# Last stage of a two-layer perceiver block: weights loaded and mixed a stage earlier, values weighted with the masked scores moving, end by batches, bias on VectorE

## The reference

```python
x = x + L0_xattn(layernorm(x), ctx)      # 16 heads over 4096 context tokens
x = x + L0_attn(layernorm(x))            # low-rank attention
x = x + L0_ffn(layernorm(x))             # 16 experts, 4 a token
x = x + L1_xattn(layernorm(x), ctx)      # top-32 attention, film, S4D, feed-forward
x = x + L1_attn(layernorm(x))            # retention, below
x = x + L1_ffn(layernorm(x))             # mixed experts, below
```

```python
# L1_attn: 8 heads of 32
Q, K, V = X @ W_Q, X @ W_K, X @ W_V      # per head
Q, K = xpos(Q), xpos(K, downscale=True)
scores = (Q @ K.T) * decay(n - m), 0 where m > n
Y = scores @ V                           # no softmax
Yn = groupnorm(Y) over each head's 32 features
Yn = Yn * gn_weight + gn_bias
out = silu(X @ W_G) * Yn @ W_O
# L1_ffn
Wsel, bsel = W[ids], b[ids]              # 8 of 32 matrices, 256x256
out = einsum('k,kod,bsd->bso', weights, Wsel, x) + einsum('k,ko->o', weights, bsel)
```

## Time and profile before

| | |
|---|---|
| median of 3 runs | 1250.7 us (1249.63 to 1252.78) |
| profiled execution | 1249.94 us, its span 1248.7 us |
| granted TensorE clock, mean over the span | 0.848 |
| TensorE busy | 1023.1 us, 82% |
| VectorE busy | 835.4 us, 67% |
| ScalarE busy | 627.9 us, 50% |
| GpSimd busy | 253.1 us, 20% |
| last stage | 1142.4 to 1248.7 us |

### The profile page before, as it was taken

The page is one execution under the profiler, slowest core; times in us unless marked ns, Lnnn a source line. Parts: engine busy times, 40 slices in busy tenths (PEclk is TensorE's granted clock), DMA queues, the critical chain, the costliest instruction groups (busy, mean ns, idle before and its releaser), DMA issues. The chain is left out here.

```text
span 1248.7 us, 20560 instructions
## 1 busy us (share of the span) xinstructions
PE 1023.1 (82%) x7560; PEld 624.6 (50%) x7560; DVE 835.4 (67%) x1812; ACT 627.9 (50%) x1014; POOL 253.1 (20%) x276
## 2 busy tenths in 40 slices
PE   6988589999999999868799782587787778973877
PEld 5877434444444444438455461335545456442564
DVE  5677689999999998036334559988485744533472
ACT  4434138787887888613311140799696882011100
POOL 1000488895000000000000010073434330000100
PEclk9999769999999999967799876667877789977855
DMA  6777522223222221010122270014521155003200
GB/s 207 273 260 270 185 66 77 78 77 84 76 76 80 76 76 39 10 53 1 52 89 76 80 187 5 1 56 115 139 78 51 39 156 186 0 1 84 68 1 17
DMA packets 97993, 110.63 MB, mean 89 GB/s; under 512 B 26475, under 2 KB 74404, under 8 KB 97892
## 3 DMA queue, kind: packets, MB, share of 16 engines
q1 hardware_dynamic: 95572, 108.52, 28.9%
q10 hardware_dynamic: 2320, 0.79, 0.3%
HBM read 79.77 MB, written 29.43 MB: 87 GB/s over the span
## 5 line engine op out<-in xcount | busy, mean ns | idle before, releaser
L806 ACT ACTIVATE pT<-bank 128x512 f32<-128x512 f32 x512 | 278.4, 597 | 94.6 <-PE bank L745 73.2
L827 DVE TENSOR_REDUCE rmax<-bank 128x2 f32<-128x1024 f32 x256 | 307.4, 1223 | 19.1 <-PE bank L713 18.1
L1547 PE MATMUL bank<-K1s,qs 97*128 97x512 f32 x256 | 137.2, 629 | 56.0 <-ACT below L1653 36.6
L757 PE MATMUL bank<-pT,V 128*17 128x256 f32 x2048 | 161.8, 388 | 4.7 <-ACT oT L812 4.6
L745 PEld LDWEIGHTS bank<-qs,ks 49*128 49x128 f32 x1024 | 78.1, 187 | 113.8 <-ACT pT L806 100.8
L1810 POOL TENSOR_TENSOR total<-total,work 128x1024 f32<-128x1024 f32 x40 | 94.7, 2375 | 194.9 <-ACT work L1662 194.5
L745 PE MATMUL bank<-qs,ks 49*128 49x256 f32 x1024 | 130.5, 333 | 2.5 <-ACT pT L806 0.5
L713 PE MATMUL bank<-ks,qs 49*128 49x512 f32 x512 | 111.2, 429 | 16.2 <-DMA ks<-k_parts_d 9.0
L1547 PEld LDWEIGHTS bank<-K1s,qs 97*128 97x128 f32 x256 | 61.1, 250 | 72.7 <-ACT below L1653 37.3
L1717 DVE MAX8 cand<-work 128x8 f32<-128x128 f32 x384 | 77.5, 279 | 0.0
L1662 ACT ACTIVATE work<-bank,ebias 128x1024 f32<-128x1024 f32 x48 | 53.6, 1120 | 31.7 <-PE bank L1550 31.7
(11 more groups left out here) (432 smaller groups left out, 1870.2 us busy)
## 6 DMA issues: line engine op xcount, KB each, us to landing
k_parts_d<-kparts SPq DMA_DIRECT2D x48, 512.0 KB, 3.6
ks<-k_parts_d SPq DMA_DIRECT2D x384, 64.0 KB, 2.2
K1s<-k_parts_d SPq DMA_DIRECT2D x96, 128.0 KB
cn<-in_ctx SPq DMA_DIRECT2D x32, 384.0 KB, 3.4
cx<-in_ctx SPq DMA_DIRECT2D x16, 384.0 KB
w<-in_L_ffn_w SPq DMA_DIRECT2D x32, 128.0 KB
w2e<-in_L_ffn_w SPq DMA_DIRECT2D x16, 128.0 KB
W<-in_L_xattn_W SPq DMA_DIRECT2D x2, 1024.0 KB, 7.4
```

The source lines that it names most:

```text
L757: t = pe.matmul(bank[32 * c:32 * c + VW, 7, a * S:(a + 1) * S], V[:, b * NCH + 4 * g + c, h, :], pT[:, (at + 2 * (c // 2) + a) % 8, c % 2 ...
L806: p_made.up(act.activation(pT[:, at % 8, :], bank[:, 4 + at % 3, :], ACT.Exp))
L827: max_read.up(dve.tensor_reduce(rmax[p % 2][:, :, qt, c], bank[:, b0:b0 + 2, :], AX.X, ALU.max))
L1547: m = pe.matmul(bank[:, b0 + c, :], qs1[0:NROW1, b * H1 + h, q], K1s[h][0:NROW1, keys], start=True, stop=(what == "new"))
```

## The change

The tiles of the last stage's loads, masks and mixed weights move to a region of SBUF that the film stage leaves free (the last 53 kB a partition), so that they can be written during it. Two new programs, `ret_load_sync` and `ret_load_pool`, run in the film stage in front of its own functions, and `mix_vector` is called in `film_vector` between the additions of `b2` and the first use of the feed-forward's result. The swapped copies are made by GpSimd. The biases of the experts are loaded to all 128 partitions. In the last stage V is the weight (32 columns, one group of columns a head) and the masked scores are the moving side; Y comes out with features on partitions and is turned back. The end runs for each batch by itself, the bias is added to `x` by VectorE, and each token tile is stored by itself.

```diff
+    phase_begins(END - 53 * 1024)
...
+    def ret_load_sync():
+        ids_in.up(sp.dma_start(ids[:, :], row("L1_ffn_ids")), 16)
+        ids_in.up(sp.dma_start(wts[:, :], row("L1_ffn_weights").to_broadcast([P, KA])), 16)
...
+        sp.wait_ge(*ids_in.at(32))
+        for k in range(KA):
+            a = sp.value_load(ids[0:1, k:k + 1], min_val=0, max_val=31)
+            wsel_in.up(sp.dma_start(wsel[:, k, :, :], ins["L1_ffn_W"][bass.ds(a, 1), :, :]
+                                    .rearrange("a (t p) d -> p (a t) d", p=P)), 16)
+            wsel_in.up(sp.dma_start(bsel[:, k, :], ins["L1_ffn_b"][bass.ds(a, 1), :].to_broadcast([P, D])), 16)
...
+    def ret_load_pool():
...
+        pool.wait_ge(*ret_in.at(16 * NRET))
+        for c in "QK":
+            for par in range(2):
+                swapped.up(pool.tensor_scalar(wsw[c][:, :, :].rearrange("p k (e two) -> p (k e) two", two=2)[:, :, par],
...
+    def mix_vector():
+        wm = wmix[:, :, :].rearrange("p t d -> p (t d)")
+        dve.wait_ge(*wsel_in.at(16 * 2 * KA))
+        vec.do(dve.tensor_scalar(wm, wsel[:, 0, :, :].rearrange("p t d -> p (t d)"), wts[:, 0:1], None, ALU.mult))
+        vec.then(dve.tensor_scalar(bmix[:, :], bsel[:, 0, :], wts[:, 0:1], None, ALU.mult))
...
+        mix_vector()
         for i in range(NT):
             dve.wait_ge(*ff_down.at(i + 1))
...
-    run(film_vector, film_scalar, film_tensor)
+    run(ret_load_sync, ret_load_pool, film_vector, film_scalar, film_tensor)
     phase_ends()
...
-        pe.wait_ge(*ret_in.at(16 * NRET))
-        pe.wait_ge(*swapped.at(4))
         pe.wait_ge(*xT_made.at(14))
...
-            for h in range(4):
-                cols = slice((4 * m + h) * DR, (4 * m + h + 1) * DR)
-                s = sR[n % 2]
-                vv = [vr[:, b * 2 + kt, cols] for kt in range(2)]
-                o = [bank[:, 4 + 2 * b + qt, cols] for qt in range(2)]
-                pe.matmul(o[0], s[:, h, 0, :], vv[0], start=True, stop=True)
-                pe.matmul(o[1], s[:, h, 1, :], vv[0], start=True, stop=False)
-                t = pe.matmul(o[1], s[:, h, 2, :], vv[1], start=False, stop=True)
+            if n >= 2:
+                pe.wait_ge(*yT_copied.at(n - 1))
+            for lo, kt, c in ((0, 0, slice(0, 2)), (P, 1, slice(2, 3))):
+                for h in range(4):
+                    cols = slice((4 * m + h) * DR, (4 * m + h + 1) * DR)
+                    t = pe.matmul(bank[h * DR:(h + 1) * DR, 4 + n % 2, lo:S], vr[:, b * 2 + kt, cols],
+                                  sR[n % 2][:, h, c, :].rearrange("p c q -> p (c q)"), start=(kt == 0), stop=(kt == 1))
             r_weighed.up(t)
+
+        def turn_back(n):
+            b, m = n // 2, n % 2
+            pe.wait_ge(*yT_copied.at(n + 1))
+            for qt in range(2):
+                t = pe.transpose(bank[:, 6 + b, qt * D + m * P:qt * D + (m + 1) * P], yT[n % 2][:, qt * P:(qt + 1) * P], ident[:, :])
+            y_turned.up(t)
...
+        for b in range(NB):
+            pe.wait_ge(*yr_made.at(b + 1))
+            turn_batch(lambda i, kt: flat(yr, i)[:, kt * P:(kt + 1) * P], b, b, yr_turned)
+            pe.wait_ge(*yrT_made.at(b + 1))
+            project_batch(wr_["O"], b, o_made)
+        for b in range(NB):
+            pe.wait_ge(*n_made.at(2 * b + 2))
+            turn_batch(tokens_of(xn), b, 2 + b, xn_turned)
+            pe.wait_ge(*xnT_made.at(b + 1))
+            project_batch(wmT, b, a_made)
...
+        for n in range(3):
+            copy_turned(n)
+        copy_back(0)
+        copy_turned(3)
+        root(0)
+        copy_back(1)
+        copy_batch(0, 0, yr_turned, yrT_made)
+        root(1)
+        copy_batch(1, 1, yr_turned, yrT_made)
...
+            for i in tiles:
+                dve.wait_ge(*n_made.at(i + 1))
+                vec.do(dve.tensor_tensor(x[:, i, :], x[:, i, :], bmix[:, :], ALU.add), biased)
+        for i in range(NT):
+            dve.wait_ge(*a_made.at(i + 1))
+            dve.wait_ge(*biased.at(i + 1))
+            out_made.up(dve.tensor_tensor(x[:, i, :], bank[:, 4 + i, 0:D], x[:, i, :], ALU.add))
```

More of the change, by code:

```diff
@@ L1813, in build @@
     phase_ends()
+    HR, DR = 8, 32
+    KA = 8
+    phase_begins(END - 53 * 1024)
+    wr_ = {c: sb(f"wr_{c}", [P, 2, D]) for c in "QKVGO"}
+    wsw = {c: sb(f"wsw_{c}", [P, 2, D]) for c in "QK"}
+    rtab = sb("rtab", [P, 4, 2, S])
+    rmask = sb("rmask", [P, 3, P])
+    gnv = sb("gnv", [P, 2, D])
+    ids = sb("ids", [1, KA], I32)
+    wts = sb("wts", [P, KA])
+    wsel = sb("wsel", [P, KA, 2, D])
+    bsel = sb("bsel", [P, KA, D])
+    wmix = sb("wmix", [P, 2, D])
+    bmix = sb("bmix", [P, D])
@@ new lines, in mix_vector @@
+    def mix_vector():
[3 more added lines that the diff above has]
+        vec.then(dve.tensor_scalar(bmix[:, :], bsel[:, 0, :], wts[:, 0:1], None, ALU.mult))
+        for k in range(1, KA):
+            vec.do(dve.scalar_tensor_tensor(wm, wsel[:, k, :, :].rearrange("p t d -> p (t d)"), wts[:, k:k + 1], wm,
+                                            ALU.mult, ALU.add))
+            vec.then(dve.scalar_tensor_tensor(bmix[:, :], bsel[:, k, :], wts[:, k:k + 1], bmix[:, :], ALU.mult, ALU.add),
+                     mixed if k == KA - 1 else None)
@@ L1989, in build @@
     sR = [sb(f"sR{j}", [P, 4, 3, P]) for j in range(2)]
+    yT = [sb(f"yT{j}", [P, S]) for j in range(2)]
     yr = sb("yr", [P, NT, HR, DR])
@@ L2059, in ret_tensor @@
                 rot_made.up(t)
+        pe.wait_ge(*wmT_made.at(2))
         for i in range(NT):
@@ L2097, in ret_tensor, with ret_scalar @@
             weigh(n)
[L2098 to L2113 removed]
+            if n:
+                turn_back(n - 1)
+        turn_back(NQD - 1)
+        for b in range(NB):
[8 more added lines that the diff above has]
+            project_batch(wmT, b, a_made)
+    def ret_scalar():
+        for kt in range(2):
+            act.wait_ge(*mix_turned.at(kt + 1))
+            wmT_made.up(act.copy(wmT[:, kt, :], bank[:, 4 + kt, 0:D]))
         norm_scalar(7)
@@ L2124, in ret_scalar, with root @@
+        def root(b):
             act.wait_ge(*gv_made.at(b + 1))
             gv_root.up(act.sqrt(gv[:, 2 * b:2 * b + 2, :], gv[:, 2 * b:2 * b + 2, :]))
[L2126 to L2154 removed]
@@ new lines, in copy_batch @@
+        def copy_batch(b, from_bank, turned_, done):
+            act.wait_ge(*turned_.at(b + 1))
+            done.up(act.copy(xT[:, :, b * S:(b + 1) * S], bank[:, from_bank, :].rearrange("p (k n) -> p k n", k=2)))
+        for n in range(3):
[7 more added lines that the diff above has]
+        copy_batch(1, 1, yr_turned, yrT_made)
+        for b in range(NB):
+            act.wait_ge(*n_var.at(b + 1))
+            n_root.up(act.sqrt(rstd[:, 2 * b:2 * b + 2], rstd[:, 2 * b:2 * b + 2]))
+            copy_batch(b, 2 + b, xn_turned, xnT_made)
@@ L2155, in ret_vector @@
+    def ret_vector():
+        norm_vector(xn, x)
+        dve.wait_ge(*swapped.at(4))
         for n, c in enumerate("QK"):
@@ L2172, in ret_vector @@
                                           ALU.mult))
-            next(mixing, None)
         def per_head(a, b):
```

165 lines of the change are left out of this document (75 added, 90 removed).

## The result

The changed kernel takes 1214.2 us (median of 4 runs, 1211.25 to 1221.8); the kernel before, run beside it, 1251.7 (1249.63 to 1254.15). The ratio is 0.971 with a 95% interval of 0.966 to 0.976: **faster**, by 37.5 us, where 1218 was forecast. A second set of runs of the same kernel gave 1214.5 and 0.970 (0.965 to 0.975).

The account below looks back on a forecast made before the run. Bounds in turn: late weight loads, TensorE, VectorE and TensorE alternating, then a serial low-clock tail. Savings 7.2 + 11.8 + 13.1 = 32.1 us from 1249.9, plus 0.8, gave 1218.6, rounded to 1218; own range 1214 to 1222, wider 1211 to 1224.

Parts of the forecast that it names:

- Loads moved: Last stage's start: projections wait only for the turned tokens, starting at 1149.06 instead of 1156.24; 7.2 us saved.
- Mixing moved: Expert-weight mixing goes into VectorE's 29.17 us feed-forward gap, with 18.8 us to spare; cost 0, under 0.5 if late.
- Rival C: Film stage: mixing waits for late expert loads and blocks the feed-forward's end; 1253 us if landing at 1158; chance 0.02, half-way 0.03.
- Projections unchanged: Last stage's projections keep their 15.77 + 6.91 + 0.91 us; clock rise may shift by 1 us.
- M to the end of the group norms: From the first mask's start, M, to the group norms' end: 24.3 us instead of 36.15, 11.8 saved.
- rival B: Values in the last stage: column groups do not overlap, 5.2 us instead of 1.7, 7.4 more, 1226; chance 0.08.
- a drain: Tiling-mode changes in the last stage: taken as 0; at 0.43 us each, the rule would give 3.9 us more.
- The tail: Group norms' end to last add: 16.5 us instead of 29.6, low clock throughout; 13.1 saved.
- a tail under 14 us: Stated sign that the forecast is wrong: the tail takes under 14 or over 18 us.
- rival A: TensorE's clock holds at 2.4 GHz through scores (1.7 us less) or returns for the last two batches (4.3 less): 1212; chance 0.16.
- Last store: Kernel's end: four small stores replace one, the last with 128 KB; 2.9 us to land, between 2 and 3.5.
- My bound for "wrong": Stated sign that the forecast is wrong: the film stage, in front of the last, grows by over 1 us.

Follow-up runs that it names:

- late_mix: The changed kernel with only the mixing back between the masks of the last stage, loads and swapped copies staying early: 1220.6 us, ratio 0.974 to the kernel before.
- old_values: The changed kernel with the values in their old form (128 weight columns, 32 moving columns, no turning back): 1222.6 us, ratio 0.977 to the kernel before.
- before_new_values: The kernel before with only the new values and turning back added; loads, mixing and tail as before: 1247.6 us, ratio 0.996.
- wait_both: The changed kernel, but TensorE starts batch 0's output projection only when both group norms are done: 1218.6 us, ratio 0.972 to the kernel before.
- warm: The changed kernel plus 20 matmuls of 512 columns, results unread, where TensorE waits: 1208.0 us, ratio 0.964 to the kernel before.
- warm_again: The changed kernel plus the same 20 unread matmuls, run once more in more rounds: 1208.8 us, ratio 0.965 to the kernel before.
- late_loads: The changed kernel with loads, swapped copies (by VectorE) and mixing back in the last stage: 1223.9 us, ratio 0.978 to the kernel before.

## Why the prediction was right, and where it was not

The sign and the three places were right, and 1214.2 is 3.8 us under the forecast, at the lower end of its own range. But the steps' sum was 8.8 us short, and the median hides that partly: with all of it the sum would have read 1209.8 us (1249.9 less 40.9, plus 0.8), under both stated ranges. That the median lies inside them is owed to the stages in front and not to the sum: luck, as far as these runs tell.

1. **Loads moved, 7.2 us.** Measured 7.17. The loads were to be in by 1082 to 1090, that is 31 to 39 us into the film stage; they were in after 29.6 us (1092.05 less 1062.48), slightly before. The copies were 2.7 us of work, near the lower end, and were not on the path.
2. **Mixing moved, cost 0.** Right, with 20.28 us of the gap left (18.8 forecast). Rival C needed loads of over 71 us (1122.5 less 1051.4); they took 29.6. late_mix shows what the move is worth: 8.8.
3. **Projections unchanged.** 23.98 against 23.70, inside the 1 us left open for the moment at which the clock rises.
4. **M to the end of the group norms, 24.3 taken, 22.37 measured**: the number worked out for the full clock, 22.6. I had chosen the value between since the stretch had been low before. old_values and before_new_values show that the form of the values decides this: 0.58 with the old, 0.85 to 0.94 with the new. Values were 0.79 us against 0.85 forecast: column groups overlap, and rival B is out (2.6; its price should have read 7.0 us, twice 5.2 less 1.7, and not 7.4). The Trainium skill (TensorEngine Tiling (Array Packing), Tiling Modes, Key Properties) states that a change of tiling mode drains the engine. The 0.79 us hold the change from column groups to the whole array and are under the forecast without a drain, so none shows in them.
5. **The tail, 16.5 forecast, 10.66 measured**: this is the mis-sized term, 5.8 of the 8.8 us, and by the forecast's own sign (a tail under 14 us) it was wrong here. The forecast's path was TensorE's own queue, three pairs of turn and projection, each priced at the low clock. They ran at the high one: 0.66 + 1.99 us in place of 1.12 + 3.47, as the timeline shows both, 1.94 a pair, 5.8 in all. TensorE does go straight on from batch 1's output projection to batch 0's expert projection, as described. But at that speed it is no longer the path: it waits 0.36 us for VectorE in front of the last turn, and the chain lies on VectorE from 1208.11 to 1214.92. Batch 0's bias adds, 0.67 us, which the forecast put beside the projections, are in that chain. "14.6 busy of 20.3 us stayed low" was read as a rule for the tail. What differed is in front of it: batch 0's output projection beside the second group norm takes the low stretch. In wait_both TensorE idles there, the first pair of the tail is low, and the tail has 0.81 and 15.96. Even there the low clock holds for one pair and not for all: the forecast priced the whole tail low. This was rival A, with a chance of 0.16; by the last stage it is the case that came true, by the median (1214.2, A said 1212) the result lies between it and the forecast.
6. **Last store, 2.9 taken, 1.75 measured**, outside my bounds of 2 to 3.5: I had a single row, for four times the size.

The sum as measured: 7.17 + 13.78 + 18.95 + 1.25 less 0.28 is 40.9. The median shows 37.5. The second profile, with no difference in front, has all 40.9; the other 3 us are within the spread of the stages in front. My bound for "wrong", a film stage longer by 1 us, was passed by one profile (92.67 against 91.07) and not by the other (91.22); it was finer than a single profile can tell. The traces show why. From the stage's start to the first matmul of L1938 (L1871 before) it takes 32.93 us in some executions and 34.3 in others, and one and the same kernel shows both (34.34 in the first profile of the changed kernel, 32.93 in the second; the same two values in warm and warm_again). In the first profile these 1.4 us lie in two groups of matmuls (L1921 4.3 us against 3.6, L1930 9.6 against 8.8), that is, in the clock. The 89.37 us of late_loads are such a step too (31.23). The rest of the stage lasts 58.14 us before and 58.15 to 58.6 in the kernels with early loads and no fillers, so beside this step the loads cost under 0.5 us. **Open** is whether they make the longer case more frequent: five of seven profiles with early loads and no fillers have it, none of the three with late loads.

## What to carry to other kernels

Price a serial tail at both clock levels and look at what TensorE does just before it: work that is hidden and therefore "worth nothing" can take the low stretch on itself. Then look at which engine the tail waits for at the faster price; here it was VectorE. Two engines that fill the same stretch must both be relieved: between M and the group norms' end the new values alone gave 5.2 us (36.15 to 30.97), the moved mixing with the old values 3.7 (36.15 to 32.49), both together 13.8. And compare stages, not totals, when executions of one program differ by 4 us.

## What the runs showed that I had not expected

- TensorE busy 93% of 26.5 us in matmuls with 32 moving columns was granted 0.58; busy 46% of 16.4 us with 128 and 256 columns, 0.94.
- Twenty matmuls whose results nobody reads made the whole kernel 6.4 us faster by the medians (1208.1 against 1214.5). Four more of them took 3.6 us back in the tail.
- A 128x16 VectorE instruction of 0.17 us took 0.81 beside a GpSimd product and ended 0.04 us after it.
